# ScalarE copies the turned context sum ahead of the last third of the turned weights

## The reference

```python
x = _layernorm(x + _L0_attn_ref(x, ...))           # x is 16 x 56 x 128
query = x @ Wq + bq
key   = ctx_768 @ Wk + bk                          # ctx_768 is 16 x 1500 x 96
value = ctx_768 @ Wv + bv
weights  = softmax(query @ key^T / sqrt(128))      # 16 x 56 x 1500
attended = weights @ value
x = _layernorm(x + attended)
x = _layernorm(x + _L0_ffn_ref(x, ...))            # 8 experts, the best 2 of each token
```

## Time and profile before

| | |
|---|---|
| median of 3 runs | 235.29 us (233.55 to 236.84) |
| the profiled execution, its own time | 235.1 us |
| its span in the trace | 233.3 us |
| mean granted clock of TensorE over the span | 0.973 |
| busy: TensorE / VectorE / ScalarE / GpSimd | 87% / 78% / 60% / 14% |

### The profile page before, as it was taken

One profiled execution on the slowest core, in us unless ns is written; L12 is line 12 of the kernel. 1 busy time (PEld: TensorE's weight loads), 2 busy tenths in 40 slices (PEclk: granted clock), 3 DMA queues, 4 the chain that ended last, 5 costly groups with the idle time before them and its releaser, 6 DMA issues. The chain is left out here.

```text
span 233.3 us, 4964 instructions
## 1 busy us (share of the span) xinstructions
PE 203.6 (87%) x1802; PEld 138.6 (59%) x1802; DVE 181.8 (78%) x430; ACT 139.4 (60%) x268; POOL 33.5 (14%) x48
## 2 busy tenths in 40 slices
PE   7899999767999877889878986999999999999920
PEld 6354555522536464566566745777787777777920
DVE  3859999987896774566776599588888888987894
ACT  2469798224534232442342645598988988898653
POOL 9472000000300001101212170000000000001520
PEclk9999999989999999999999997999999999999995
DMA  5999999006630988693611100031121301000002
GB/s 150 317 234 275 273 239 318 22 0 154 158 85 7 312 262 220 233 238 134 215 37 48 45 3 0 0 93 46 49 48 42 90 9 36 0 0 3 0 0 80
DMA packets 7808, 26.11 MB, mean 112 GB/s; under 512 B 928, under 2 KB 1312, under 8 KB 7792
## 3 DMA queue, kind: packets, MB, share of 16 engines
q1 hardware_dynamic: 7792, 25.89, 39.4%
HBM read 25.43 MB, written 0.46 MB: 111 GB/s over the span
## 5 line engine op out<-in xcount | busy, mean ns | idle before, releaser
L839 ACT ACTIVATE terms<-bank,b_now 128x448 f16<-128x448 f32 x64 | 40.6, 634 | 12.7 <-PE bank L551 12.7
L572 PE MATMUL bank<-w2h,terms 128*128 128x128 f16 x256 | 44.4, 219 | 0.0
L572 PE MATMUL bank<-w2l,terms 128*128 128x128 f16 x256 | 44.3, 219 | 0.0
L572 PE MATMUL bank<-w2h,sums 128*128 128x128 f16 x256 | 44.3, 219 | 0.0
L1226 DVE TENSOR_TENSOR sums<-pc,terms 128x448 f16<-128x448 f32 x60 | 37.0, 620 | 9.4 <-ACT pc L847 9.4
L847 ACT ACTIVATE pc<-bank,b_now 128x448 f32<-128x448 f32 x64 | 40.6, 635 | 0.0
L551 PE MATMUL bank<-turned_late,w1h 128*128 128x448 f16 x128 | 34.7, 353 | 0.0
L572 PEld LDWEIGHTS bank<-w2h,terms 128*128 128x128 f16 x256 | 25.0, 98 | 4.8 <-issue 2.9
L572 PEld LDWEIGHTS bank<-w2l,terms 128*128 128x128 f16 x256 | 25.0, 98 | 1.9
L439 PE MATMUL bank<-ctxT_slot,w_conv 97*64 97x500 f32 (+1 forms) x96 | 23.5, 629 | 1.9 <-ACT pc L763 1.4
L572 PEld LDWEIGHTS bank<-w2h,sums 128*128 128x128 f16 x256 | 25.0, 98 | 0.0
(11 more groups left out here) (173 smaller groups left out, 343.9 us busy)
## 6 DMA issues: line engine op xcount, KB each, us to landing
ctx_slot<-ctx SPq DMA_DIRECT2D x16, 576.0 KB, 5.3
ctxT_slot<-ctx_T SPq DMA_DIRECT2D x16, 562.5 KB, 8.2
w_raw<-w SPq DMA_DIRECT2D x16, 256.0 KB, 2.6
convw_sb<-conv_w SPq DMA_DIRECT2D x3, 256.0 KB, 6.0
small_sb<-small SPq DMA_DIRECT2D x1, 609.0 KB, 9.6
xpad<-x_T SPq DMA_DIRECT2D x2, 236.0 KB, 5.5
xtok<-x_tok SPq DMA_DIRECT2D x1, 448.0 KB, 11.2
out<-x SPq DMA_DIRECT2D x2, 224.0 KB, 2.3
```

What stands on the lines that cost most here:

```text
L572: mm = pe.matmul(bank[:, to, j * D:(j + 1) * D], h_[:, s, f, i, :], w_[:, s, f, :], start=(f == 0 and k == 0), stop=(f == FC - 1 and k == 2))
L839: nc.scalar.activation(hh[:, s, f, c * PPH:(c + 1) * PPH, 0:PT], bank[:, n % 4, 0:HW] .rearrange("p (j t) -> p j t", j=PPH), ACT.Relu, sca ...
```

## The change

On ScalarE, `turned_sum(i - 1)` now stands in front of `turned_copy(i)`. In turn 2 it is thereby in front of `queried_keys(2)` too.

```diff
@@ -785,6 +785,8 @@
                     factor(1)
                 if i == 2:
                     x1T_copy(2)
+                if i:
+                    turned_sum(i - 1)
                 turned_copy(i)
                 if i == 0:
                     square(1, M, M + 2)
@@ -792,7 +794,6 @@
                 if i == 2:
                     queried_keys(2)
                 if i:
-                    turned_sum(i - 1)
                     if i == 1:
                         mix_inv_std(2)
                     attended_inv_std(i - 1)
```

## The result

| | before | changed |
|---|---|---|
| median of 6 runs each | 234.93 us | 231.25 us |
| lowest to highest | 233.55 to 236.84 | 226.30 to 233.23 |
| the profiled execution, its span | 235.1, 233.3 | 232.84, 231.1 |
| its mean granted clock | 0.973 | 0.953 |

The ratio is 0.969, with an interval of 0.959 to 0.979: faster, by 7.2 us of 234.9. The runs of a kernel that lie over 1.5% above its lowest are left out of that ratio; that took out three of the six runs of the changed kernel (232.84, 232.96, 233.23) and none of before, and the profile shown here is of one of those three.

What follows compares the result with a forecast made beforehand. TensorE, busy 203.6 of 233.3 us, was taken to bound the kernel. Gains of 0.62 (turn 2), 0.80 (turn 3), 3 x 0.76 and 0.80 (turn 7) sum to 4.50, from 235.1 to 230.6 us; range 228.8 to 232.5.

Steps and rivals of the forecast that it cites:

- What waits, and that it goes: TensorE's values waited six times, 5.3 us in total, for ScalarE's copy of the turned sum; the change removes that wait.
- Turns 4 to 6: Small copy starts about 0.10 us after the accumulator read's start, so TensorE gains 0.76 us per turn, 2.28 in all.
- Rival A: In turns 4 to 6 ScalarE frees late, small copy starts at 103.96; gain 0.46 us each, time 231.5; chance 0.12.
- Turn 2: Values come 1.33 us earlier, but the scores of turn 3 wait about 0.7 us for the queried keys; gain 0.62.
- Rival B: Turn 2 is won in full because queried keys don't hold the scores; sum 5.2 us, time 229.9; chance 0.05.
- The prediction's sign for B: Scores of turn 3 starting ahead of 88.8 us would mean that the queried keys don't hold them.
- Turns 3 and 7: ScalarE is not held there, so the whole wait of 0.80 us goes in each, 1.60 together.
- The rest follows: Behind the values nothing becomes late: slack 0.7 us for the exponential, 0.37 for VectorE, 5.9 for loads; gain carries undiminished.
- D: Another wait replaces the removed one in every turn, such as the exponential or VectorE's copies; 234 to 235 us; chance 0.05.
- E: Copy of the last third comes so late that the next turn's context sum waits; slower, 236.9 us; chance 0.03.
- the sum: Gains over turns 2 to 7 in attention add up to 4.50 us, for a time of 230.6 us.
- rival C: Clock falls around 142 to 146 us, costing up to 1.7; one less gives 228.9, one more 232.3; chance 0.20.

Runs made afterwards that it cites:

- e9: Changed kernel with the old order in turn 2 alone, plus warming matmuls sized to three TensorE pauses; 227.76 us, on another chip than e7.
- e2: Changed kernel with ScalarE's copy of the queried keys also ahead of the last third in turn 2; median 227.02 us, ratio 0.963 to before.
- e8: Changed kernel with the queried keys also ahead of the last third in turn 2, plus the warming matmuls of e6; 226.34 us, ratio 0.964 to before.
- e6: Kernel before, with 4, 3 and 7 more warming matmuls in three TensorE pauses, sized to fit them; 231.86 us (231.52 to 232.25).
- e7: Changed kernel with the same warming matmuls as e6; 226.96 us (226.67 to 227.19).

## Why the prediction was right in its mechanism and wrong in its verdict

*What waits, and that it goes.* Right: the values' waits went in all six turns, and nothing took their place but what was named.

*Turns 4 to 6.* 0.78 us each against 0.76. Rival A (ScalarE comes free late) falls: the small copy starts 0.09 after the read's start in each of them. The prediction took the 0.09 from the earlier trace rows as "the same two instructions". They are not: there the queried keys follow the read, not this copy, so that carrying the number over was partly luck. The small copy behind a read is what this case now shows at 0.09 us.

The Trainium skill, page "Perfetto Trace Analysis", section "DVE / Act Engine Instruction", lets the next instruction begin to fetch when the one before has finished executing, and has the profiled end lie later, at the acknowledgement of its last write. So the rule does not put the copy behind the read's profiled end, as the prediction had it. The copy at 101.30, within the read that runs from 101.21 to 101.40, neither contradicts it nor bears it out, since no row shows when the read had finished executing.

*Turn 2.* Right in mechanism: the scores waited 0.76 us for the queried keys (0.7 was forecast). Turns 1 and 2 together gained 0.61, forecast 0.62; e9 puts turn 2 at 0.59 and e2 and e8 show the wait to be the keys'. Rival B falls. The prediction's sign for B, scores of turn 3 ahead of 88.8, did come up (88.23), but only because it was a time on the clock of the old profile: from the first scores on, it is 39.40 us here, where 88.91 - 49.52 = 39.39 was forecast.

*Turns 3 and 7: the terms that were mis-sized.* Forecast 0.80 each, "only some hundredths larger" at most; measured 1.05 and 0.89. I took the idle time in the row of the values as the whole of the wait. It counts from the modelled end of the last third, and with its data ready the values start ahead of that end: 94.85 against 94.32 + 0.70 = 95.02 in turn 3, 120.16 against 120.25 in turn 7. These are the last thirds of turns 3 and 7 in the trace of before:

```profile
95.62 0.69 PE L449 MATMUL bank<-small_sb,convw_sb 120*125 120x120 f32 x4 [0.21 <-DVE ph L1168]
...
124.34 0.60 PE L449 MATMUL bank<-small_sb,convw_sb 120*125 120x120 f32 x4
```

From the start of the last third to the values it was 1.49 and 1.40 us before, and is 0.53 and 0.51 now. In turn 3 the scores also follow the values after 0.41 instead of 0.50. These 0.34 us, with 0.02 in each of three turns, are the difference of 4.89 to 4.50 (within 0.01, from turns 1 and 2). In turn 3 ScalarE was also held, against the prediction: the turned sum is done at 94.11 in that trace and its copy starts at 94.25, 0.09 after the start of the accumulator read. It cost nothing, since 94.25 + 0.31 = 94.56 is ahead of 94.85.

*The rest follows.* Right: VectorE kept 0.35 us (0.37 forecast), no load was late, the gain reached the router weights undiminished (4.90), and rivals D and E did not occur.

*The verdict.* I forecast 230.6 us and, with 0.54, a result within 2%. The median came at 231.25, inside the range, but the ratio is faster by 3.1%, clear of its interval. Two steps failed. The first is the sum: 4.90 is 2.1% of 235 and 4.50 was 1.9%, and I let the chances hang on a line that lay within the error of my own terms. The second is larger: rival C. It allowed one half-speed stretch more or less at 1.7 us each, and knew of one only. The profile of before held two, worth 1.7 and 1.6 us, so that a run without any is 3.3 us faster, not 1.7. And a stretch can be three times as long: 4.9 us behind the router weights, 2.6 at the first scores. Measured were runs of the changed kernel 8.3 us apart (226.30 to 234.60, over both sets) around the same work.

The ratio of 0.969 compares 227.6 us, the mean of 226.30, 226.90 and 229.66, with 234.85, the mean of the six runs of before, and so reads 7.2 us for a change of 4.9. The mean of all six runs of the changed kernel is 230.3, which is 4.5 us or 1.9% less. With the pauses filled, the same two orders stand at 226.96 and 231.86, a ratio of 0.979. So the order by itself lies at about 2%, on the line between the two verdicts, and what the ratio shows beyond it goes with the clock (0.987, 0.986 and 0.971 in its three runs, 0.973 in the profile of before).

*What stays open.* Four of the thirteen unwarmed runs of the changed kernel had a mean clock of 0.986 or more, as the warmed kernels have it (0.982 to 0.990). I take these for runs without any stretch, though no trace of one was kept. Two of the four runs of e2 had it too. None of the 30 runs of before whose clock is recorded came above 0.980 (one more, of 535.31 us, is left aside here). Whether the shift by 4.9 us makes such runs possible was not tried. Nor is it shown what ends a long stretch, since TensorE was busy all through it, or which of the three groups of warming matmuls prevents which fall, since they were only added together.

## What to carry to other kernels

Where a wait for a short copy is behind a longer one on the same engine, look at which input is there first, and then follow the consumer one step further: in turn 2 the next matmul needed a copy that had not moved, and moving that too gave 0.62 us more (0.76 in the traces). The idle time that a TensorE row shows need not be the whole wait, since it counts from a modelled end: in turns 3 and 7 it was 0.80, and the values came 0.96 and 0.89 us sooner. The distance between starts, compared with the same pair where nothing waits, is the better term. Where runs of one kernel spread by more than the effect, look at the granted clock of each run, and fill the pauses ahead of the falls before a small gain is weighed: in e6 that took the spread from 5.3 us to 0.7, and made the kernel before 3.2 us faster.

## What the runs showed that was not expected

The lower clock level can last long under work: 10 us (137.6 to 147.9 in the changed kernel's profile) with TensorE busy without a gap, behind a pause of 2.82 us. By the Trainium skill, page "TensorE: Matmul & The Clock Gate", section "What's actually happening", activity lifts the clock again. The trace agrees for the stretch of 3.4 us in the kernel before, and that of the changed kernel has one three times as long with TensorE just as busy. With fourteen additional passes of 0.19 us in the pause of 2.82 us, and the two other groups, the clock stood at 1.00 in e6, e7 and e8. Nothing was lost by it: the router weights' turning still had 0.18 us to wait for VectorE behind the last of them. And the copy behind an accumulator read of 0.19 us on ScalarE starts 0.09 us after the start of that read.
